# Keys by head part, a turned edge, value bias at the turned outputs, and the first MoE's first layer with gathered rows stationary

## The reference

```python
x = x + tanh(g_xattn[0]) * L0_xattn(layernorm(x), ctx)   # each head sees every 16th context row
x = x + tanh(g_ffn[0])   * L0_ffn(layernorm(x))          # 8 experts, each takes its best 64 tokens
x = x + tanh(g_xattn[1]) * L1_xattn(layernorm(x), ctx)   # full attention, 16 heads, 512 keys
x = x + tanh(g_ffn[1])   * L1_ffn(layernorm(x))          # 16 experts, top 1, and a shared MLP

# in both attentions: Q = x@Wq + bq, K = c@Wk + bk, V = c@Wv + bv, softmax(QK/sqrt(8)) V, then @Wo + bo
# L0_ffn:
scores = softmax(xf @ gate_w.T)                  # (512, 8)
vals, idx = top_k(scores.T, 64)                  # per expert
y = layernorm(xf[idx]) * ln_w + ln_b
h = gelu(einsum('knd,nfd->knf', y, fc1s) + b1s)  # 128 -> 512
out = (einsum('knf,ndf->knd', h, fc2s) + b2s) * vals
xf = xf.at[idx].add(out)
```

## Time and profile before

| | us |
|---|---|
| median of three runs | 169.97 |
| time of the profiled execution | 169.73 |
| its span | 167.9 |
| TensorE busy | 151.3 |
| VectorE busy | 108.7 |
| ScalarE busy | 86.7 |
| GpSimd busy | 65.5 |

### The profile page before, as it was taken

One profiled execution on the slowest core, in us unless ns is written; L12 is line 12 of the kernel. 1 busy time (PEld: TensorE's weight loads), 2 busy tenths in 40 slices (PEclk: granted clock), 3 DMA queues, 4 the chain that ended last, 5 costly groups with the idle time before them and its releaser, 6 DMA issues.

```text
span 167.9 us, 3337 instructions
## 1 busy us (share of the span) xinstructions
PE 151.3 (90%) x1229; PEld 105.5 (63%) x1234; DVE 108.7 (65%) x316; ACT 86.7 (52%) x159; POOL 65.5 (39%) x100
## 2 busy tenths in 40 slices
PE   7799997797999989898799999999898999898993
PEld 2357884744389985674355555554554778498993
DVE  0777768896923447799997797797142668742052
ACT  3142646761128304556987797797797536602010
POOL 7589936687893524069950000000021342100000
PEclk9999999789599999999999999999999999999999
DMA  5999960004386789001152000000000700000002
GB/s 154 327 302 422 433 234 2 0 2 117 76 187 133 156 178 382 29 0 46 40 76 35 0 0 4 0 0 0 4 0 4 252 0 2 0 4 0 4 0 70
DMA packets 4294, 15.43 MB, mean 92 GB/s; under 512 B 948, under 2 KB 1844, under 8 KB 3492
## 3 DMA queue, kind: packets, MB, share of 16 engines
q1 hardware_dynamic: 2980, 11.66, 22.9%
q10 hardware_dynamic: 576, 2.44, 4.3%
q0 software_dynamic: 720, 1.09, 3.1%
HBM read 13.94 MB, written 1.25 MB: 90 GB/s over the span
## 4 chain that ended last, share of the span: by engine, by line
PE 63%; DVE 10%; POOL 8%; ACT 8%; DMA 5%; issue 4%; ACTq 0%; POOLq 0%; DVEq 0%
PE bank L522 59%; PE bank L526 4%; DMA fc1T_sb<-q_rows 3%; POOL fc1T_sb L479 2%; POOL q_rows L474 2%; ACT arena L1154 2%; ACT fc1T_sb L1162 2%; DVE top L1338 2%; DVE k L1340 2%; DMA x_sb<-in_x 2%; POOL xb L403 1%; DVE kpack L1563 1%; PE bank L699 1%; PE bank L1012 1%; POOL rstd L384 0%
## 5 line engine op out<-in xcount | busy, mean ns | idle before, releaser
L1466 DVE TENSOR_REDUCE mx<-bank 128x1 f32<-128x512 f32 x64 | 40.9, 684 | 6.1 <-PE bank L522 6.1
L1154 ACT ACTIVATE arena<-bank 128x1024 f32<-128x1024 f32 x32 | 31.1, 1030 | 1.5 <-PE bank L522 1.3
L522 PE MATMUL bank<-kpack,fc1T_sb 72*128 72x512 bf16 x64 | 22.8, 382 | 1.7 <-DVE mx L1466 0.7
L380 POOL TENSOR_SCALAR rstd<-meanvar 128x2 f32<-128x2 f32 x10 | 2.2, 222 | 50.6 <-DVE meanvar L1243 49.1
L522 PE MATMUL bank<-fc1T_sb,kpack 104*128 104x256 bf16 x128 | 19.3, 273 | 1.2 <-ACT arena L1154 0.6
L522 PE MATMUL bank<-arena,va 128*32 128x256 f32 x256 | 15.5, 382 | 0.5 <-ACT arena L1154 0.5
L522 PEld LDWEIGHTS bank<-fc1T_sb,kpack 104*128 104x128 bf16 x128 | 11.8, 97 | 6.5 <-ACT arena L1154 1.7
L522 PEld LDWEIGHTS bank<-kpack,fc1T_sb 72*128 72x128 bf16 x64 | 6.1, 96 | 9.6 <-issue 3.6
L1162 ACT CAST fc1T_sb<-bank 8x1024 bf16<-8x1024 f32 x8 | 8.0, 1005 | 7.3 <-PE bank L522 7.2
L522 PEld LDWEIGHTS bank<-arena,va 128*32 128x32 f32 x256 | 7.5, 109 | 6.8 <-ACT arena L1154 1.9
L522 PE MATMUL bank<-selq_bf,zeros_bf 128*128 128x512 bf16 (+1 forms) x33 | 9.4, 429 | 0.5 <-issue 0.3
(11 more groups left out here) (253 smaller groups left out, 301.6 us busy)
## 6 DMA issues: line engine op xcount, KB each, us to landing
kpack<-k_parts SPq DMA_DIRECT2D x3, 768.0 KB
fc1T_sb<-in_fc1T SPq DMA_DIRECT2D x1, 2048.0 KB, 13.2
fc_sb<-in_fc SPq DMA_DIRECT2D x1, 2048.0 KB, 17.4
fc_sb<-in_gateup ACTq DMA_DIRECT2D x2, 1024.0 KB, 9.2
arena<-in_down SPq DMA_DIRECT2D x1, 1024.0 KB, 4.8
k_parts<-arena SPq DMA_DIRECT2D x8, 96.0 KB, 2.2
fc1T_sb<-q_rows POOLq DMA_DIRECT2D x9, 64.0 KB, 2.9
ctxT_sb<-in_ctxT SPq DMA_DIRECT2D x2, 256.0 KB, 4.8
```

Source lines behind the costliest of these rows:

```text
L380: pool.tensor_scalar(rstd[:, k, i:i + 2].unsqueeze(2), meanvar[:, k, i:i + 2, 1:2], EPS, None, ALU.add)\
L522: return pe.matmul(o, lhsT, rhs, start=start, stop=stop, **k)
L1154: act.activation(probs1[:, n % (2 * GH), :, :], bank[:, 2 + 2 * (n % 2):4 + 2 * (n % 2), :], ACT.Exp, scale=SCALE)\
L1466: dve.tensor_reduce(mx1[:, b * 2 + qt, g * GH + j:g * GH + j + 1], bank[:, r, :], AX_X, ALU.max)\
```

## The change

- Keys by head part. `wkey_rows` is Wk with its columns in the order place in head, head; `ident_rows` is the identity in that order. ScalarE makes both with two copies, in the place of the copy of the bias. The keys then come out in the order in which they are stored, and SyncE writes them in three transfers, each sent when its part is there. The bias vector is turned by one product with `ident_rows` into bank 7 and copied to `bkcol`. The subtractions on GpSimd go by halves.
- Value bias at the turned outputs. `bvcol` and the four products of the two `bias` rows are gone. The value bias is added where ScalarE copies the turned outputs out (`attT`), since the weights of the softmax sum to one; `bo` is loaded to all partitions (`rows_sb`, now a 128 KB transfer on SyncE's queue).
- First attention on TensorE: all queries ahead of all scores, the value products between the transposes of the probabilities. ScalarE's Tanh of the gates moves behind the queries, a Tanh of a constant stands first in its place.
- Turned edge. One transpose of `edge`, broadcast along its row, brings it to all partitions (bank 6). VectorE compares `score` with it twice into `marks`; TensorE counts in eight products of 64, 48, 32, 16 and four times 32 columns. The runs of products with zeros are 24 and 5.
- `yn` is made by ScalarE (scale and bias), GpSimd only makes its bias `mean_gone`. The split of `score` moves behind the masks. A Gelu of a constant stands ahead of the copies of `sel0T`.
- First layer. `yT` of an expert (64 columns) is stationary, its weights stream 512 columns wide, two experts in the halves of the output partitions: 8 fp32 products. `rows0` is copied out (VectorE for c = 0, 1, 3, ScalarE for 2), turned back by 16 fp32 transposes, the bias is added from the turned banks, and gelu and the second layer follow. The kept scores are made between the first layer's c = 1 and the transposes.

The core of the diff:

```diff
@@ sync
+            sp.dma_start(rows_sb[:], rows.to_broadcast([P, 2, D])).then_inc(L["rows"], 16)
...
-            sp.wait_ge(S["k3_sb"], 1)
-            for d in range(DH):
-                sp.dma_start(krows[:, d, :, :].rearrange("j h s -> h j s"), k3[d:P:DH, :, :]).then_inc(S["scr_out"], 16)
-            sp.wait_ge(S["scr_out"], 16 * DH)
+            sp.wait_ge(S["k1_hi"], NB)
+            sp.dma_start(kparts[0, :, :], k3[:, 0, :]).then_inc(S["scr_out"], 16)
+            sp.wait_ge(S["k1_mid"], NB)
+            sp.dma_start(kparts[1, :, :], k3[:, 1, :]).then_inc(S["scr_out"], 16)
+            sp.wait_ge(S["k3_sb"], NB)
+            sp.dma_start(kparts[2, :, :], k3[:, 2, :]).then_inc(S["scr_out"], 16)
+            sp.wait_ge(S["scr_out"], 16 * 3)
@@ gpsimd
+            ln_rstd(4, 0)
+            mean_gone_of(0)
+            ln_rstd(4, 2)
+            for b in range(NB):
+                pool.wait_ge(S["k1_hi"], b + 1)
+                pool.tensor_tensor(k1r[:, keys_half(b)], k1[:, keys_half(b)], k3[:, 0, keys_half(b)], ALU.subtract)\
+                    .then_inc(S["k1_rest"], 1)
+            mean_gone_of(2)
...
-            pool.wait_ge(S["score_sb"], 1)
+            pool.wait_ge(S["sel0_sb"], NT)
             link(pool.tensor_copy(score3[:, :, 0, :], score[:]))
@@ tensor
             probs0_turned(0)
+            values0(0)
             probs0_turned(1)
+            values0(1)
             weighted0(0)
...
+            pe.wait_ge(S["k1_sb"], 2)
             for b in range(NB):
-                mm(bank[:, b, :], w1_sb[:, 1, :], ctxT_sb[:, b * SK:(b + 1) * SK]).then_inc(S["k1_ps"], 1)
+                mm(bank[:, b, :], wkey_rows[:], ctxT_sb[:, b * SK:(b + 1) * SK]).then_inc(S["k1_ps"], 1)
...
+            mm(bank[:, 7, 0:1], ident_rows[:], vec(V_BK1)).then_inc(S["k1_ps"], 1)
...
-            keep_running(21, 7)
-            pe.wait_ge(S["gradeT_sb"], 1)
+            keep_running(24, 7)
+            pe.wait_ge(S["edge_sb"], 1)
+            transpose(bank[:, 6, 0:HE], edge[:].to_broadcast([HE, P]), HE).then_inc(S["edge_ps"], 1)
...
+            pe.wait_ge(S["marks_sb"], 1)
+            ranks = bank[:, 7, 0:NT * 2 * E0].rearrange("p (i m e) -> p i m e", m=2, e=E0)
+            mm(ranks, tri_bf[:], marks[:], stop=False)
+            for k in range(NT - 1):
+                mm(ranks[:, k + 1:, :, :], ones_bf[:], marks[:, k:k + 1, :, :].to_broadcast([P, NT - 1 - k, 2, E0]),
+                   start=False, stop=False)
+            for k in range(NT):
+                ins = mm(ranks[:, :, 1, :], ones_bf[:], marks[:, k:k + 1, 0, :].to_broadcast([P, NT, E0]),
+                         start=False, stop=k == NT - 1)
+            ins.then_inc(S["cum0_ps"], 1)
+            keep_running(5, 4)
...
+            def first_layer(c):
+                for u in range(2):
+                    e = 2 * c + u
+                    ins = mm(bank[u * CAP0:(u + 1) * CAP0, SCB[c], :], yT[:, e * CAP0:(e + 1) * CAP0], fc1T_sb[:, e, :])
+                ins.then_inc(S["fc1_ps"], 1)
+            def rows0_turned(c):
+                if c == 2:
+                    pe.wait_ge(S["rows0_act"], 1)
+                else:
+                    pe.wait_ge(S["rows0_sb"], min(c, 2) + 1)
+                for f in range(FC0):
+                    ins = transpose(bank[:, TURNB[c], f * P:(f + 1) * P], rows0[:, c, f * P:(f + 1) * P])
+                ins.then_inc(S["rows0T_ps"], 1)
...
+            first_layer(0)
+            first_layer(1)
+            pe.wait_ge(S["sel0T_sb"], PR0)
+            pe.wait_ge(S["score3_sb"], 1)
...
+            rows0_turned(0)
+            first_layer(2)
+            rows0_turned(1)
+            first_layer(3)
+            rows0_turned(2)
+            pe.wait_ge(L["fc2"], 16)
+            pe.wait_ge(S["kept_sb"], 1)
+            second_layer(0)
+            rows0_turned(3)
+            for c in range(1, PR0):
+                second_layer(c)
@@ scalar
+                    act.copy(wkey_rows[:].rearrange("p (d h) -> p d h", d=DH), w1_sb[:, 1, :].rearrange("p (h d) -> p d h", d=DH))\
+                        .then_inc(S["k1_sb"], 1)
...
+            act.wait_ge(S["k3_sb"], NB)
+            act.wait_ge(S["fc1_ps"], 3)
+            act.copy(rows0[:, 2, :], bank[:, SCB[2], :]).then_inc(S["rows0_act"], 1)
@@ vector
+            for m, test in ((0, ALU.is_gt), (1, ALU.is_equal)):
+                ins = dve.tensor_tensor(marks[:, :, m, :].rearrange("p (h i) e -> p h i e", h=2), score_now, edge_now, test)
...
+            dve.wait_ge(S["k3_sb"], NB)
+            rows0_copied(0)
+            rows0_copied(1)
...
+            hidden_bias(0)
...
+            hidden_bias(1)
+            rows0_copied(3)
+            hidden_bias(2)
+            hidden_bias(3)
```

More of the change, by code:

```diff
@@ L215, in build @@
         edge = sb("edge", [HE, 1])
[L216 to L221, removed]
+        marks = sb("marks", [P, NT, 2, E0], BF16)
+        slots = sb("slots", [P, NT, 2, E0])
         slot0 = sb("slot0", [P, NT, E0], BF16)
@@ L554, in _, with values0 @@
                    zeros_bf[:].unsqueeze(1).to_broadcast([P, T // P, P]))
+            def values0(b):
+                for c in range(b * KC, (b + 1) * KC):
+                    mm(bank[:, 2 + b, (c % KC) * P:(c % KC + 1) * P], ctxT_sb[:, c * P:(c + 1) * P],
+                       w0_sb[:, 2, :]).then_inc(S["v0_ps"], 1)
             pe.wait_ge(L["const"], 16)
@@ L656, in _ @@
-            ins.then_inc(S["grade_ps"], 1)
-            def count_before(pb, mask, n, at=0, ahead=None):
-                for i in range(NT):
-                    o = bank[:, pb, at + i * n:at + (i + 1) * n]
-                    first = True
-                    for k in range(NT if ahead is not None else 0):
-                        mm(o, ones_bf[:], ahead[:, k, :], start=first, stop=False)
-                        first = False
+            keep_running(24, 7)
+            pe.wait_ge(S["edge_sb"], 1)
@@ L687, in _ @@
             ins.then_inc(S["yT_ps"], 1)
[L688 to L695 removed]
+            pe.wait_ge(S["k1_sb"], NB + 3)
             pe.wait_ge(S["va1_sb"], NB * KC)
@@ L723, in _ @@
                 ins.then_inc(S["fc2_ps"], 1)
+            first_layer(0)
+            first_layer(1)
+            pe.wait_ge(S["sel0T_sb"], PR0)
+            pe.wait_ge(S["score3_sb"], 1)
+            for k in range(PR0):
+                for i in range(NT):
+                    ins = mm(bank[:, KEPTB, k * 3 * E0:(k + 1) * 3 * E0], sel0[:, i, 2 * k:2 * k + 2, :],
+                             score3[:, i % 2 * 2 + i // 2, :, :], start=i == 0, stop=i == NT - 1)
+            ins.then_inc(S["kept_ps"], 1)
@@ L1059, in _ @@
             act.copy(probs0T[:, NT - 1, :], bank[:, NT - 1, :]).then_inc(S["p0T_sb"], 1)
-            copies("attT0_ps", "attT0_sb", lambda i: attT[0][:, i, :], lambda i: bank[:, i, 0:P])
+            for i in range(NT):
+                act.wait_ge(S["attT0_ps"], i + 1)
+                act.activation(attT[0][:, i, :], bank[:, i, 0:P], ACT.Identity, bias=vec(V_BV)).then_inc(S["attT0_sb"], 1)
             def centred(i):
@@ L1105, in _ @@
                          .rearrange("p (h d) -> p h d", d=DH)).then_inc(S["va1_sb"], 1)
-            act.wait_ge(S["bias_ps"], 2)
-            act.copy(bias[:, 1, :], bank[:, 6, 0:D]).then_inc(S["bias_sb"], 1)
-            act.wait_ge(S["yn_sb"], NT)
-            act.copy(yn3[:, 0, :, :], yn[:]).then_inc(S["yn_p1"], 1)
+            for c in range(KC):
+                values_copied(c)
             act.wait_ge(S["yn_r1"], 1)
             act.copy(yn3[:, 1, :, :], ynr[:]).then_inc(S["yn_p2"], 1)
+            for c in range(KC, NB * KC):
+                values_copied(c)
+            act.activation(sig[:, 2, :], gates_sb[:], ACT.Gelu_apprx_tanh)
             act.wait_ge(S["sel0T_ps"], NT)
```

218 lines of the change are left out of this document (95 added, 123 removed).

## The result

| | before | changed |
|---|---|---|
| median, us | 169.56 (4 executions, 169.10 to 170.08) | 164.68 (4 executions, 164.50 to 164.71) |
| profiled execution | 169.73 | 164.50 |
| its span | 167.9 | 162.7 |

The changed kernel takes 0.9709 of the time of the one before (95% interval 0.9672 to 0.9747): 4.9 us less in the medians, 5.2 us less between the two profiled executions. The forecast was 165.6, its own range 164.3 to 166.6. A ratio takes in only the executions within 1.5% of the fastest of their kernel, which leaves two out in e10 and none elsewhere.

A forecast was written before the change was run, and what follows sets the result against it. Bound: TensorE's order in the first attention, then a VectorE-TensorE relay to the second layer's end. Terms +0.2 - 0.8 - 1.45 - 1.5 - 0.8 = -4.35 took 169.73 to 165.4, median 165.6; own range 164.3 to 166.6, 8 in 10 164.0 to 167.4.

The forecast's parts named there:

- What bounds the kernel: TensorE's order in the first attention, then a VectorE-TensorE relay from edge to second layer's end; the rest moves with that end.
- First attention: From first scores to first weighted sum: TensorE's work falls from 8.3 to 7.4 us; -0.8 us (0 to -1.2).
- Bias product: Turning the key bias puts two more fp32 records ahead of the router's products: +0.2 us (0 to +0.3).
- Ranking: Edge to first mask takes 2.1 us, with 0.3 waiting for products with zeros, instead of 3.55: -1.45 (-0.8 to -1.9).
- Masks and gathering: First mask to last gathering product takes 3.5 us instead of 5.0, at full clock: -1.5 (0 to -1.9).
- First layer: Last gathering product to second layer's end takes 11.3 us instead of 12.1, pairs running at once: -0.8 (+3.0 to -1.3).
- rival 2: The first layer's pairs run one after the other, 7.5 us instead of 4.1: 169.0 us in all; chance 0.07.
- ScalarE's copies of the turned masks end before the kept scores are due: In the first MoE's first layer: these copies, 2.05 us, end before TensorE comes to the kept scores.
- Keys: Keys by head part: sending the transfers back earlier buys nothing, 0, since their first reader leaves 20 us of room.
- Rival 4: Behind the second layer, a later stage waits for something that did not move and loses gain: 167 to 170 us; chance 0.07.
- Rival 1: The clock still falls after the ranking; masks and gathering give 0.3 instead of 1.5: 166.8 us; chance 0.13.
- Rival 3: The clock falls in the first layer and stays down until the second ends: about 176 us; chance 0.03.

The follow-up runs named there:

- e10: Changed kernel with the keys' transfers back sent at about 46.4 us instead of 37.5: 167.16, 168.25, 164.46 and 165.53 us, median 166.35; ratio 0.9731 from the last two.
- e5: Changed kernel with TensorE's old order in the first attention, the bias row still gone: 165.77 us, ratio 0.9781.
- e6: Changed kernel with the product that turns the key bias moved ahead of the last transpose of `nT1`, where TensorE waits: 164.45 us, ratio 0.9705.
- e13: e8 run again, on the same chip as e11: 164.06 us, ratio 0.9678.
- e12: e8 with all four first-layer pairs in a row, then kept scores, then all sixteen transposes; ScalarE copies blocks 2 and 3: 163.77 us, ratio 0.9655.
- e1: Changed kernel with 10 instead of 24 products with zeros ahead of the edge's transpose: 166.03 us, ratio 0.9792.
- e9: Changed kernel with the old ranking (marks in the turned layout, 36 counts) and 24 products with zeros ahead of it: 166.36 us, ratio 0.9814.
- e3: Changed kernel with GpSimd's last subtraction of the split of `yn` held until the counts are done: 165.83 us, ratio 0.9812.
- e2: Kernel before the change with 24 instead of 21 products with zeros ahead of the transposes of the marks: 169.16 us, ratio 0.9987.
- e8: Changed kernel with the key bias product as in e6, masks turned and copied block by block, and 23 products with zeros: 164.10 us, ratio 0.9688.
- e11: Changed kernel unaltered, run again on another chip: 164.47 us, ratio 0.9706.

## Why the prediction was right, and where its steps were not

**What bounds the kernel** held. The relay of small pieces set the time, and the 108 us behind it moved as one block.

**First attention: -1.91, forecast -0.8, bound -1.2. The largest error.** I added rows at full length, and a row of the timeline ends after the next one has begun. From 9.51 us, where the first score started before, to the first weighted sum there are now 6.43 us, where my sum had 7.4: 0.34 instead of 0.5 for the queries ahead, 3.43 from the scores' start to that of the next group instead of 3.8, 2.66 instead of 3.09 for transposes and values. The chain counts each piece up to the next and would have given the right lengths. And I looked for TensorE's work that goes; of the 1.0 that the new order gives nothing is work, it is waiting for ScalarE (e5).

**Bias product: +0.27, forecast +0.2.** Right, and avoidable only in part (e6).

**Ranking: -1.74, forecast -1.45.** Edge to first mask is 1.81 us where the walk gave 2.1. Each piece came out near its price (marks 0.30 instead of 0.4, counts 0.37 for 0.4); the last product of zeros did hold the edge back, by 0.13 us (0.43 from the edge to the marks, where e13's trace has 0.30) instead of 0.3. This wait is not the same in each execution. Timeline of VectorE and windows of TensorE in e12, and the window of e13:

```profile
38.47 0.28 DVE L1398 TENSOR_TENSOR marks<-score,bank 128x32 bf16<-128x32 f32 x2 [1.06 <-PE bank L533]
```

```profile
29.00:33.00 4.00, 3.78 (x18) 0.50 0.18 66
```

```profile
29.00:33.00 4.00, 3.95 (x22) 0.73 0.18 66
```

In e12 the half clock of the first dip lasted longer, and even with 23 products of zeros the marks started 1.06 us after the edge, 0.76 later than in e13. That is the price of what e1 shows these products bring. No number of them suits every execution: where the first dip is long they hold the edge back (e12), where it is missing they end early and leave TensorE idle (e9).

**Masks and gathering: -1.43, forecast -1.5.** Four masks took 2.50 us where I had 2.8, the last product ended 1.1 behind them and not 0.7: full clock, no collision. e1 prices the clock at 1.4, e3 the collision at 0.9 to 1.1, and e2 shows that in the kernel before they were not a sum.

The Trainium skill (GPSIMD Engine Reference, section Specifications) has the rule that I weighed here, contention with VectorE instructions that have two SBUF inputs. I had held against it that only the first mask was slow. e2 and e3 agree with the rule for the instruction that starts beside the two-input operation; and where a small operation of GpSimd meets a mask, the other engine pays. The same cast in e2, beside the masks, and in the changed kernel, behind them:

```profile
44.50 0.55 POOL L447 CAST score<-score_hi 128x32 bf16<-128x32 f32 x1
```

```profile
42.56 0.21 POOL L456 CAST score<-score_hi 128x32 bf16<-128x32 f32 x1
```

**First layer: -0.4, forecast -0.8.** The mechanism was right and rival 2 is out: eight records in 1.94 us, and in e12 all sixteen in 3.65, half of the 7.5 in line. The stage takes 11.7 us instead of 11.3, and the terms that were mis-sized are the transposes, 0.49 + 0.59 + 0.58 + 0.59 = 2.25 instead of 1.8, the kept scores, 0.56 instead of 0.4, and the second layer, 3.8 instead of 3.7; the pairs were better than priced (3.96 for 4.1). Four transposes that stand between half-width products take 0.59 us where they took 0.44 in the first attention, and the weight loading of the pair behind them has its own idle piece, in the changed kernel's timeline:

```profile
46.99 0.20 PEld L529 LDWEIGHTS bank<-fc1T_sb,arena 128*64 128x64 f32 x4 [0.17 <-issue]
```

The Trainium skill (TensorEngine Tiling (Array Packing), section Key Properties) says that changing the tiling mode drains TensorE; these rows agree, and put it at about 0.15 us for each group of transposes between two pairs, that is for two changes.

The step "ScalarE's copies of the turned masks end before the kept scores are due" was wrong too, by little: the pairs ended at 45.82 and the kept scores began at 46.02. The chain puts 2.06 us down to these copies; of this only 0.2 is TensorE's idle time, which was within the 0.35 that I had set aside for waits, and e8 got 0.3 back.

The Trainium skill (TensorE: Matmul & The Clock Gate, section Measured speedup vs the span model) was the source of the estimate beside this term, the first layer in 4.7 us. e12's 3.65 decides against it: two column tiles gave the full factor.

**Keys: the number was right by luck, the reason wrong.** I read 20 us of room from the time of sending and the first reader, and forgot the transfer's own length. In the changed kernel the transfer back is sent at 37.5 us, and the windows show when the queues fall silent:

```profile
46.00:52.00 6.00, 5.98 (x60) 1.00 0.74 156
52.00:53.00 1.00, 1.00 (x22) 1.00 0.14 33
```

So it lasts some 14 us (37.5 to 52), and in e10, beside the experts' load, 18. The room was 9 us at most, and the stages ahead of the reader have lost 5. Sending the keys earlier brings no time by itself, but e10 says that at the old time they could come too late for the faster stages. How late the old way of storing them would have sent them in the changed kernel was not run. Rival 4 was thus nearer than its 0.07.

**Rival 1** did not come true: no second fall in the trace. **Rival 3** neither: from 43 to 55 us, half-width layer and transposes, the mean clock was 1.00.

**The sum.** Terms +0.27 - 1.91 - 1.74 - 1.43 - 0.4 = -5.2 against -4.35: two steps gave 1.4 more, one 0.4 less. The total was nearer than its parts.

## What to carry to other kernels

Where TensorE is fed by a relay, sum a new order from the pieces of the chain, not from row lengths, and count the waits that the new neighbours fill. Before you price the removal of one delay, look for a second one that it covers: clock and collision here cost 1.4 and 0.9 to 1.1 us one by one in the changed kernel, and removing the clock's fall alone from the old kernel brought nothing that can be told. The room of a transfer is its reader's start less its sending less its own duration beside whatever shares the queues.

## What the runs showed of the hardware that was not expected

- A VectorE instruction with two SBUF inputs that met a two-input operation of GpSimd of 128x512 (1.15 us) got done only behind it, however small it was: a 128x32 operation of 0.19 us took 1.01 and 1.19 us (e3, e2). GpSimd's 128x2 operation of the layer norm held nothing back: in the kernel before it ran from 28.89 to 29.61 us, and the subtraction of the softmax (line 1321, both inputs in SBUF) began inside it, at 29.25, and took its usual 0.19.
- The clock after one and the same softmax wait differs between executions: half from 29.2 to 32.4 us in the changed kernel's trace, full in those of e1 and e9, and a mean of 0.50 and 0.73 from 29 to 33 us in those of e12 and e13, whose instructions are the same up to there and kept TensorE busy for 0.68 us of 26.5 to 28.9 in both. Two of e11's six executions have a mean granted clock of 1.00, no dip at all, and took 164.66 and 164.36 us, the other four 164.06 to 165.18: under the ranking, where VectorE sets the pace, a dip of that length costs nothing that can be told; the longer one of e12 held the edge back by 0.76.
- A single idle wait of 1.71 us ahead of the second attention was followed by half clock in a stage that shows it in no other trace (e10).
